# A graph layer's last stage: selecting products one trip later, and the self term added by an accumulating transfer

## What is computed

```
h  = relu(layernorm(x))
x1 = x + segment_sum(h[src] * weight, dst) @ W_neigh + b_neigh + h @ W_self.T
s, m, a = segment sum, max, mean of edge_attr over edges with the same src
x2 = x1 + relu(concat(s, m, a, u) @ W1 + b1) @ W2 + b2
```

## Time and profile before

| | |
|---|---|
| median of 3 runs | 1773.02 us (1772.13 to 1776.54) |
| the profiled execution | 1769.93 us, its span 1768.0 us |
| busy in the span | PE 1081.4, DVE 1390.8, ACT 679.9, POOL 1104.8 us |
| DMA | 255.33 MB in 433690 packets, 373693 of them under 512 B |
| last stage | from about 1075 us to 1760 us |

### The profile page before, as it was taken

How to read it: one execution, slowest core, us unless ns; L and a number is a source line. 1 busy time by engine, 2 the same in 40 slices (tenths; PEclk the granted TensorE clock), 3 DMA queues, 4 the chain that set the end, 5 groups by cost and what they waited for, 6 DMA issues and landing times. The chain is left out here.

```text
span 1768.0 us, 39354 instructions
## 1 busy us (share of the span) xinstructions
PE 1081.4 (61%) x13658; PEld 933.2 (53%) x13659; DVE 1390.8 (79%) x3220; ACT 679.9 (38%) x1766; POOL 1104.8 (62%) x1407
## 2 busy tenths in 40 slices
PE   3266666666651023333333344898989998999996
PEld 2155555555551023332233333777877777777775
DVE  6599999999981056766667666888888988888886
ACT  2278888888840012222222221333333333333332
POOL 7777777777777777777777755444444444444440
PEclk9777788888865555555555556888788888878787
DMA  9944545454531053344432226878887878787882
GB/s 289 169 115 116 128 113 128 115 129 114 130 101 42 15 128 96 104 111 106 108 103 71 85 84 166 211 203 206 198 211 194 211 195 206 206 201 201 203 204 61
DMA packets 433690, 255.33 MB, mean 144 GB/s; under 512 B 373693, under 2 KB 381117, under 8 KB 432813
## 3 DMA queue, kind: packets, MB, share of 16 engines
q1 hardware_dynamic: 283198, 144.42, 33.7%
q0 software_dynamic: 46976, 72.79, 15.8%
q10 hardware_dynamic: 103312, 35.54, 8.0%
HBM read 164.15 MB, written 88.42 MB: 143 GB/s over the span
## 5 line engine op out<-in xcount | busy, mean ns | idle before, releaser
L850 POOL DMA_INDIRECT xg_all<-in_x_dram,idx_src x391 | 397.9, 1018 | 120.1 <-issue 118.9
L856 POOL DMA_INDIRECT by_win<-rows,idx_win x391 | 388.1, 993 | 128.1 <-issue 127.2
L1185 PE MATMUL ps<-ident,h 128*128 128x128 f32 x588 | 139.9, 384 | 279.0 <-DVE h L999 204.9
L1413 POOL DMA_DIRECT2D rows<-by_win x98 | 67.7, 691 | 353.9 <-DVE arena L1444 333.2
L1271 ACT ACTIVATE sq<-xc 128x512 f32<-128x512 f32 x147 | 92.6, 630 | 472.5 <-DVE xc L962 472.4
L1185 PEld LDWEIGHTS ps<-ident,h 128*128 128x128 f32 x588 | 94.7, 198 | 298.9 <-DVE h L999 218.2
L951 DVE TENSOR_REDUCE stat<-xg_all 128x8 f32<-128x512 f32 x49 | 33.4, 682 | 230.4 <-DMA xg_all<-in_x_dram,idx_src 230.3
L1418 POOL DMA_DIRECT2D rows<-flag_d x392 | 193.6, 501 | 12.2 <-issue 12.2
L1289 ACT ACTIVATE h<-xc,stat 128x64 f32<-128x64 f32 x784 | 196.3, 332 | 0.0
L1629 ACT ACTIVATE arena<-ps 96x512 bf16<-96x512 f32 x98 | 58.0, 592 | 332.9 <-PE ps L1568 238.1
L1568 PE MATMUL ps<-w_sb,arena 128*96 128x64 f32 x1568 | 184.1, 281 | 0.0
(11 more groups left out here) (209 smaller groups left out, 2580.4 us busy)
## 6 DMA issues: line engine op xcount, KB each, us to landing
rows<-message SPq DMA_DIRECT2D x784, 36.4 KB, 3.3
rows<-flag_d POOLq DMA_DIRECT2D x392, 72.0 KB, 3.6
rows<-s_d SPq DMA_DIRECT2D x98, 256.0 KB, 2.9
out_dram<-rows ACTq DMA_DIRECT2D x97, 256.0 KB
message<-m_row SPq DMA_DIRECT2D x48, 388.0 KB, 2.4
arena<-in_x_dram SPq DMA_DIRECT2D x70, 256.0 KB, 3.4
s_d<-arena SPq DMA_DIRECT2D x70, 256.0 KB, 2.2
zeros<-slot_d POOLq DMA_DIRECT2D x98, 144.0 KB, 3.3
```

The lines of the kernel that those rows point to most:

```text
L850: nc.gpsimd.indirect_dma_start(out=xg[g % RX][:, t % GT, :], out_offset=None, in_=x, in_offset=bass.IndirectOffsetOnAxis(ap=idx_src[:, t:t ...
L856: nc.gpsimd.indirect_dma_start(out=by_win, out_offset=bass.IndirectOffsetOnAxis(ap=idx_win[0:parts, t:t + 1], axis=0), in_=rows[0:parts, t ...
L1185: last = nc.tensor.transpose(hT_of[n % 2][:, P * k:P * k + P], h[n % 2][:, 2 * k:2 * k + 2, :].rearrange("p a c -> p (a c)"), ident[:, :])
```

## The change

The scratch table goes. The first stage stores the self term of a group straight into `out`, with `nodes_of`. In the last stage nothing loads it; the final DVE addition becomes a copy from PSUM to `y` on ACT (`finish`, in the place of `store`), and POOL adds `y` to `out` with an accumulating transfer, six groups behind its loads. `edges` moves from g-1 to g-2, and `v_part` exists twice.

```diff
-        s0_d = dram("s0_d", [WG * GT * P, D])
...
                     if kind == "node":
-                        sp.dma_start(self_of(g), xs[g % XR][:, :, :]).then_inc(xs_out[g % XR], 16)
+                        if g == WG - 1:
+                            full, short = last_nodes(out)
...
+                        else:
+                            sp.dma_start(nodes_of(out, g), xs[g % XR][:, :, :]).then_inc(xs_out[g % XR], 16)
...
-        v_part = parts_of(part_of(arena, SL, GT, KEY))
+        v_part = [parts_of(part_of(arena, SL, GT, KEY)) for _ in range(2)]
...
                     sp.reg_load(at, starts[0:1, 0, g * GT:g * GT + GT])
-                    if g >= RING:
-                        sp.wait_ge(w["y"], g - RING + 1)
-                    sp.dma_start(x_in[b][:, :, :], self_of(g)).then_inc(x_loaded[b], 16)
...
+                def add_to_out(g):
+                    b = g % RING
+                    pool.wait_ge(w["y"], g + 1)
+                    if g == WG - 1:
...
+                    else:
+                        pool.dma_start(nodes_of(out, g), y[b][:, :, :], accum_op=ALU.add).then_inc(summed_out[b], 16)
+
+                STORE_LAG = 6
                 for g in range(WG):
                     load(g)
+                    if g >= STORE_LAG:
+                        add_to_out(g - STORE_LAG)
+                for g in range(WG - STORE_LAG, WG):
+                    add_to_out(g)
...
-                def finish(g):
-                    b = g % RING
-                    dve.wait_ge(w["o_ps"], g + 1)
-                    dve.wait_ge(x_loaded[b], x_before[b] + nth(g) * 16)
-                    if g >= RING:
-                        dve.wait_ge(stored[b], x_before[b] + (nth(g) - 1) * 16)
-                    nc.vector.tensor_tensor(y[b][:, :, :], x_in[b][:, :, :],
-                                            ps[o_bank[g % 2]][:, :].rearrange("p (k c) -> p k c", c=D),
-                                            ALU.add).then_inc(w["y"], 1)
-
                 def value_left(g):
                     dve.wait_ge(w["high"], g + 1)
+                    if g >= 1:
+                        dve.wait_ge(w["v"], g)
...
-                    if g >= 1:
-                        finish(g - 1)
                 value_left(WG - 1)
                 value_low(WG - 1)
-                finish(WG - 1)
...
-                    if g >= 1:
-                        edges(g - 1)
+                    if g >= 2:
+                        edges(g - 2)
                     outer(g)
                     neighbours(g)
+                edges(WG - 2)
                 edges(WG - 1)
...
-                def store(g):
+                def finish(g):
                     b = g % RING
-                    act.wait_ge(w["y"], g + 1)
...
+                    act.wait_ge(w["o_ps"], g + 1)
+                    if g >= RING:
+                        act.wait_ge(summed_out[b], 16 * (g // RING))
+                    nc.scalar.activation(y[b][:, :, :], ps[o_bank[g % 2]][:, :].rearrange("p (k c) -> p k c", c=D),
+                                         ACT.Copy).then_inc(w["y"], 1)
...
                 def value_high(g):
                     act.wait_ge(w["v_ps"], g + 1)
-                    if g >= 1:
-                        act.wait_ge(w["o_ps"], g)
+                    if g >= 2:
+                        act.wait_ge(w["o_ps"], g - 1)
...
                     relu(g)
                     if g >= 2:
-                        store(g - 2)
+                        finish(g - 2)
                     value_high(g)
```

More of the change, by code:

```diff
@@ L270, in ranking @@
         def ranking(name, *more):
-            return {s: sem(f"{name}_{s}") for s in ("oh", "eq", "same", "h", "t", "ohT", "w", "begin", "look", "idx", *more)}
+            return {s: sem(f"{name}_{s}") for s in ("oh", "eq", "same", "t", "ohT", "w", "begin", "look", "idx", *more)}
         def digits_of(own, name, code):
@@ L648, in graph_layers @@
         win_sent = sem("win_sent")
-        r_win, r_dst = ranking("rank_win", "read"), ranking("rank_dst", "done", "h_used", "t_used")
+        r_win, r_dst = ranking("rank_win", "read"), ranking("rank_dst", "h", "done", "h_used", "t_used")
         hg = {s: sem(f"hist_{s}") for s in ("oh", "used", "rows", "base")}
@@ L744, in store @@
                     if kind == "node":
-                        sp.dma_start(self_of(g), xs[g % XR][:, :, :]).then_inc(xs_out[g % XR], 16)
+                        if g == WG - 1:
+                            full, short = last_nodes(out)
+                            sp.dma_start(full, xs[g % XR][:, 0:WR, :]).then_inc(xs_out[g % XR], 16)
+                            sp.dma_start(short, xs[g % XR][0:N % P, WR, :]).then_inc(xs_out[g % XR], 16)
+                        else:
+                            sp.dma_start(nodes_of(out, g), xs[g % XR][:, :, :]).then_inc(xs_out[g % XR], 16)
                         if g + NODES_AHEAD + 1 < WG:
@@ L793, in _ @@
                 for b in range(XR):
-                    sp.wait_ge(xs_out[b], 16 * len(range(b, WG, XR)))
+                    sp.wait_ge(xs_out[b], 16 * (len(range(b, WG, XR)) + (b == (WG - 1) % XR)))
                 for b in range(2):
@@ L1381, in graph_layers @@
                                           "left", "mid", "v", "sel", "pick", "picked", "o_ps", "y")}
-        x_loaded, stored = xs_here[0:RING], xs_out[0:RING]
-        x_before = [16 * len(range(b, WG, XR)) for b in range(RING)]
+        summed_out = [sem(f"win_summed_out{b}") for b in range(RING)]
         ch_loaded = [sem(f"win_ch_loaded{b}") for b in range(RING)]
@@ L1419, in load @@
                                        two.unsqueeze(0).to_broadcast([DE, 3 * 2 * SL])).then_inc(a_loaded[b], 16)
+                def add_to_out(g):
+                    b = g % RING
+                    pool.wait_ge(w["y"], g + 1)
+                    if g == WG - 1:
+                        full, short = last_nodes(out)
+                        pool.dma_start(full, y[b][:, 0:WR, :], accum_op=ALU.add).then_inc(summed_out[b], 16)
+                        pool.dma_start(short, y[b][0:N % P, WR, :], accum_op=ALU.add).then_inc(summed_out[b], 16)
+                    else:
+                        pool.dma_start(nodes_of(out, g), y[b][:, :, :], accum_op=ALU.add).then_inc(summed_out[b], 16)
+                STORE_LAG = 6
                 for g in range(WG):
                     load(g)
+                    if g >= STORE_LAG:
+                        add_to_out(g - STORE_LAG)
+                for g in range(WG - STORE_LAG, WG):
+                    add_to_out(g)
+                for b in range(RING):
+                    pool.wait_ge(summed_out[b], 16 * (len(range(b, WG, RING)) + (b == (WG - 1) % RING)))
             @block.vector
@@ L1588, in edges @@
                         for n in range(PARTS):
-                            last = nc.tensor.matmul(ps[o_bank[c]][:, D * k:D * k + D], sel[c][:, k, :], v_part[:, k, n, :],
+                            last = nc.tensor.matmul(ps[o_bank[c]][:, D * k:D * k + D], sel[c][:, k, :], v_part[c][:, k, n, :],
                                                     start=False, stop=(k == GT - 1 and n == PARTS - 1))
@@ L1626, in value_high @@
                     act.wait_ge(w["v_ps"], g + 1)
-                    if g >= 1:
-                        act.wait_ge(w["o_ps"], g)
-                    nc.scalar.activation(v_part[:, :, 0, :], ps[v_bank][0:SL, :].rearrange("p (k c) -> p k c", c=D), ACT.Copy).then_inc(w["high"], 1)
+                    if g >= 2:
+                        act.wait_ge(w["o_ps"], g - 1)
+                    nc.scalar.activation(v_part[g % 2][:, :, 0, :], ps[v_bank][0:SL, :].rearrange("p (k c) -> p k c", c=D), ACT.Copy).then_inc(w["high"], 1)
                 def value_mid(g):
                     act.wait_ge(w["left"], g + 1)
-                    nc.scalar.activation(v_part[:, :, 1, :], v_left[:, :, :], ACT.Copy).then_inc(w["mid"], 1)
+                    nc.scalar.activation(v_part[g % 2][:, :, 1, :], v_left[:, :, :], ACT.Copy).then_inc(w["mid"], 1)
                 for g in range(WG):
@@ L1639, in _ @@
                     if g >= 2:
-                        store(g - 2)
+                        finish(g - 2)
                     value_high(g)
                 value_mid(WG - 1)
[L1643 to L1646, removed]
+                finish(WG - 2)
+                finish(WG - 1)
         more = {n: sem(f"more_{n}") for n in ("longest", "in", "near", "pick", "ps", "y", "out")}
```

13 lines of the change are left out of this document (2 added, 11 removed).

## The result

The changed kernel takes 1639.49 us in the median of four runs (1638.38 to 1642.61) against 1772.58 us before: a ratio of 0.9248, 95% interval 0.9229 to 0.9267, 133 us less. The forecast was 1668 with a range from 1640 to 1745, so the direction and the mechanism came true, and the time lies 28.5 us under the forecast, half a microsecond under the range.

A forecast was written before the change was run, and what follows sets the result against it. DVE bounds the last stage's trip at the full clock, PE at the low one. 97 x (6.80 - 5.70) = 107 us less, +2 at the end, takes 1769.9 to 1665; the median, 3.1 above, is 1668, range 1640 to 1745.

The forecast's parts named there:

- The wait on the selecting products: On PE in the last stage: its 1.03 us wait goes, and 0.3 us of idling ahead of the output product replaces it.
- DVE's loop of 5.37 us: Last stage: without the final addition (0.60 us) and its only hole (0.17), DVE's trip falls from 6.14 to 5.37 us.
- The clock stays high: Last stage: denser PE work keeps the clock nearly always at 1.00; trips of 5.4 to 6.0 us, 1639 to 1697, chance 0.50.
- Four that meet in one trip don't mesh without loss, and I add 0.3: 5.7 us: Last-stage trip: DVE 5.37, PE 5.4, SP 4.6 to 5.4 and DMA 5.0 us, with 0.3 added for meshing.
- my 5.4: PE's predicted trip in the last stage, 5.4 us with its wait on ACT's ReLU, 5.1 without.
- The lower end of the range: Whole kernel: 1639 us at trips of 5.4 us, in the case of a high clock with chance 0.50; stated range from 1640.
- SP's 4.6 to 5.4 us: SP's queue in the last stage: eight message loads and register loads per trip, without the self term's load.
- POOL's issue: POOL's queue in the last stage: one more issue of 1024 pieces per trip, 0.9 us, making 3.1 us per trip 4.0.
- The accumulate's 1.8 us of the engines: DMA engines per last-stage trip: adding transfer 1.8 us at POOL's packed rate with both operands read; with 3.2 remaining, 5.0.
- my estimate by that rule, 5.6 us per trip: DMA engines in the last stage: adding at half the plain store's rate, 3.2 + 2.4 = 5.6 us, would make them the bound.
- The first stage: Storing the self term in 1024 pieces of 256 bytes instead of 2 KB ones: counted as nothing, 3 us either way.
- The end: After the last trip: a 0.6 us copy, then POOL's issue and an adding transfer instead of ACT's; +2 us, between 0 and +5.

The follow-up runs named there:

- PE filled: The kernel before with seven useless products on PE ahead of the selecting products; ratio to before 0.9688, last stage 621.2 us against 686.0.
- one pick: The changed kernel with the subtraction ahead of the picks folded into them as one DVE instruction; 1643.37 us, ratio to before 0.9273.
- accumulating alone: The changed kernel with the selecting products back at one trip behind, copy on ACT and accumulating transfer kept; ratio to before 1.0048, last stage 692.2 us.

## Why the prediction was right and where it was wrong

- **The wait on the selecting products** goes, and a short one ahead of the output product takes its place: right. I gave it 0.3 us; it is 0.17.
- **DVE's loop of 5.37 us:** right, 5.35.
- **The clock stays high:** right, 1.00. That PE's hole drives it was only argued then; PE filled shows it for the kernel before. The Trainium skill ("TensorE: Matmul & The Clock Gate", on the HAM clock gate) says that activity releases the lower clock, and this case agrees: useless products alone took the clock from 0.83 to 1.00.
- **"Four that meet in one trip don't mesh without loss, and I add 0.3: 5.7 us":** this is the step that failed. The trip is 5.35, 5.32 in the mean of the copy's intervals. DVE and SP both need just that, and hardly anything is lost by their meeting. The 0.3 had no row behind it. It is 29 us of 97 trips; with the 0.05 to 0.08 by which the trip is also under my 5.4 it makes 37 us too much. The loss I had in mind does appear once DVE is faster than SP (one pick: 33 intervals over 5.45).
- **What lies outside the 97 intervals** hid part of that: it takes 39.2 us (555.5 - 516.3) where it took 26.6 (686.0 - 659.4), 12.6 more, and I had counted 2. The first copy comes 7.4 us later in the stage than the first addition did, which I had put at nothing; the selecting products come a trip later, but accumulating alone has 27.4 us there too, so the lag isn't all of it. The end has the other 5.2. The remaining 4 us of the miss are the step from the traced execution to the median, 3.1 us up before and 0.7 down after.
- **The lower end of the range,** 1639 for trips of 5.4, is what was measured, by luck: the trips are 0.08 us shorter than that (8 us), and the stage's start and end take 10.6 us more.
- **SP's 4.6 to 5.4 us:** right at its upper end. Between 1150 and 1600 us its groups of eight loads take from 4.6 to 6.3 us from start to start, 5.4 in the mean, and DVE still waits for no message: the ring of four groups evens it out.
- **POOL's issue** at 0.9 us for 1024 pieces: 0.94 when plain, 1.68 when adding. The price of the row was right for a store, and adding doubles it. It was covered, as POOL had the room (305.6 of 350 us busy, 4.7 of 5.35).
- **The accumulate's 1.8 us of the engines:** 3.2 us by its records, over the 2.4 of the plain store's rate twice. I took POOL's packed rate, and adding transfers aren't packed. POOL's queue went up by 66 points of share (26.2 to 92.5), where I had named less than 25 as a sign of being right. By my count the sum would then be 6.4 us and the DMA engines the bound; they weren't. The other half of that step was wrong too: the shares of the changed kernel add up to 1.23 of the engines' time, so records overlap and a sum of shares is no occupation. The Trainium skill ("Collectives: The Full Stack", the section on the fold count and the bandwidth ceiling) says that the reduce step of a ring runs at half the rate because it reads two sources; my estimate by that rule, 5.6 us per trip with the DMA engines as the bound, isn't what this case shows. The records lengthen by more than two (3.2 us against 1.2), and the time by nothing.
- **The first stage** at nothing: 0.8 us.
- **The end** at +2 us, between 0 and +5: +5.2 (8.8 against 3.6), just over that. Plain transfers from POOL didn't shorten it, transfers from SP and ACT did.

## What to carry to other kernels

Where the trace shows TensorE at the lower clock for part of a stage, measure what the clock alone is worth by filling its wait with useless products; here that took one edit and showed half of the gain. Don't add a charge for several engines being near their limit without a row for it: here they run ahead of one another through rings, and the trip was the longest one's sum. Count what lies outside the trips by itself: a stage's first result and its end moved by 12.6 us here. When the first limit is removed, look for a queue without waits (here SP's) before taking more off the busiest engine, and expect edits that pay more in pairs than alone.

## What I had not expected of the hardware

- An adding transfer of 1024 pieces of 256 bytes costs GpSimd 1.68 us to issue and one packet a piece; the same transfer stored plainly 0.94 us and about 80 packets.
- A subtraction of 96x8 takes 0.15 us on DVE and 1.05 us on POOL in this stage.
- The permutation on DVE takes 609 ns, and 493 ns behind a memset on DVE.
- A second transfer of 1024 pieces in ACT's queue held ACT in its issue for up to 7.2 us; with one per trip no issue took over 0.44 us.
